# A GNN kernel's fused node pass: straight code for 196 groups on four engines in place of loops of 20 steps

## The reference, cut to what matters

```python
h = jnp.maximum(_layernorm(x, axis=-1), 0.0)
x = x + _L0_gnn_ref(h, edge_index, Ws, att_src, att_dst, bias)    # 3 layers: x + sigmoid(gat_conv(x))
h = jnp.maximum(_layernorm(x, axis=-1), 0.0)
x = x + _L1_gnn_ref(edge_index, h, edge_weight, We0, be0, Wn0, bn0, ...)   # 3 layers
```

## Time and profile before

| what | value |
|---|---|
| time, median of 3 runs | 6525.8 us (6522.49 to 6534.74) |
| time of the profiled execution | 6529.22 us |
| its span, first to last instruction | 6527.7 us |
| busy over the span: PE, DVE, ACT, POOL | 4932.6, 4483.4, 3646.1, 4296.6 us (76, 69, 56, 66%) |
| node pass, 62 to 2007 us: PE, DVE, ACT, POOL busy | 1746.0, 1502.8, 1658.4, 1414.3 of 1945 us |
| granted TensorE clock, mean over the span | 0.878 |

### The profile page before, as it was taken

How to read it: one execution, slowest core, us unless ns; L and a number is a source line. 1 busy time by engine, 2 the same in 40 slices (tenths; PEclk the granted TensorE clock), 3 DMA queues, 4 the chain that set the end, 5 groups by cost and what they waited for, 6 DMA issues and landing times. The chain is left out here.

```text
span 6527.7 us, 110704 instructions
## 1 busy us (share of the span) xinstructions
PE 4932.6 (76%) x23310; PEld 3004.7 (46%) x23310; DVE 4483.4 (69%) x12803; ACT 3646.1 (56%) x7987; POOL 4296.6 (66%) x4317
## 2 busy tenths in 40 slices
PE   4999999999984557847783666059989997776665
PEld 2665555655651134424442444036656664333332
DVE  6887877877865868858885899866655554444443
ACT  4998888988875736645662444753333332333332
POOL 4777777777730077737755775047767775777777
PEclk9999999999998968877886555579999998999998
DMA  6888878777754556646663777877767774444442
GB/s 197 269 277 270 267 261 279 249 223 224 227 185 162 189 149 199 200 126 188 203 203 121 227 231 233 258 212 223 222 202 237 235 234 147 131 129 129 126 124 91
DMA packets 889075, 1314.93 MB, mean 201 GB/s; under 512 B 294247, under 2 KB 347208, under 8 KB 882092
## 3 DMA queue, kind: packets, MB, share of 16 engines
q1 hardware_dynamic: 745906, 1077.42, 49.7%
q0 software_dynamic: 142688, 232.29, 15.1%
HBM read 660.03 MB, written 654.88 MB: 201 GB/s over the span
## 5 line engine op out<-in xcount | busy, mean ns | idle before, releaser
L1304 POOL DMA_INDIRECT g_xs<-table,g_gi x1176 | 1240.1, 1055 | 919.8 <-DMA g_gi<-in_src_lookups_dram 399.4
L1632 POOL DMA_INDIRECT n_xs<-table,n_gi x1176 | 1204.3, 1024 | 727.7 <-DMA n_gi<-lookups 358.2
L1775 DVE TENSOR_TENSOR_SCAN n_dT<-n_km,n_dT,bank 128x512 f32<-128x512 uint8 x291 | 372.4, 1280 | 1007.6 <-PE bank L1660 997.0
L1735 ACT ACTIVATE n_eT<-bank,edge_b 128x512 f32<-128x512 f32 x294 | 202.1, 688 | 803.0 <-PE bank L1677 797.2
L698 PE MATMUL bank<-n_zT,wn 128*128 128x512 f32 (+1 forms) x1176 | 542.7, 597 | 82.9 <-ACT n_sg L756 59.8
L679 PE MATMUL bank<-n_xT,gat_w 128*128 128x512 f32 (+1 forms) x1176 | 561.9, 615 | 54.0 <-issue 34.9
L1643 POOL DMA_INDIRECT out_dram<-n_xn,n_eo x392 | 432.3, 1103 | 124.8 <-issue 113.3
L619 POOL DMA_INDIRECT node_map<-p_es x392 | 401.1, 1023 | 119.5 <-issue 116.5
L647 POOL DMA_INDIRECT p_lk<-node_map,p_gi x392 | 391.3, 998 | 128.2 <-issue 106.1
L1179 DVE CUSTOM_DVE_ANT_0 g_junk<-g_xs,v_src 128x128 f32<-128x128 f32 x1176 | 272.9, 284 | 294.7 <-DMA g_xs<-table,g_gi 293.9
L614 POOL DMA_INDIRECT p_rows<-in_x_dram,p_es x392 | 393.0, 1003 | 124.8 <-issue 113.3
(11 more groups left out here) (253 smaller groups left out, 12292.2 us busy)
## 6 DMA issues: line engine op xcount, KB each, us to landing
table<-n_ro SPq DMA_DIRECT2D x768, 256.0 KB
g_gb<-decays SPq DMA_DIRECT2D x294, 256.0 KB, 4.1
n_xd<-table SPq DMA_DIRECT2D x294, 256.0 KB
table<-g_xn SPq DMA_DIRECT2D x196, 256.0 KB
g_xo<-table SPq DMA_DIRECT2D x196, 256.0 KB
edge_feats<-n_eT SPq DMA_DIRECT2D x196, 256.0 KB, 2.8
table<-n_xn SPq DMA_DIRECT2D x196, 256.0 KB
n_ea<-edge_feats SPq DMA_DIRECT2D x196, 256.0 KB
```

Source lines behind the costliest of these rows:

```text
L1304: q.indirect_dma_start(out=xs[g % XR][:, u, :], out_offset=None, in_=tables[l], in_offset=bass.IndirectOffsetOnAxis(ap=gi[g % 6][:, 0, u:u ...
L1632: q.indirect_dma_start(out=xs[g][:, u, :], out_offset=None, in_=tables[L], in_offset=bass.IndirectOffsetOnAxis(ap=gi[g][:, u, slot_word:sl ...
L1775: V.tensor_tensor_scan(in_order(dT[g][:, :]), kept(g), in_order(flat_banks[1]), 0.0 if begins(g) else carry(dT[g.before(1)]), ALU.mult, AL ...
```

## The change

`unrolled` takes the place of `pipeline` for PE, ACT, DVE and SP in the node pass. It writes all steps out, so that `Turn.i` is None throughout: every address and every count of a wait is a constant, and there is no `Fori`, no branch and no register arithmetic. GpSimd's two pipelines and those of all later passes stay. The parameter `last_peeled` goes. Line numbers behind L80 grow by 10.

```diff
-def pipeline(eng, groups, work, un, base=0, last_peeled=0):
+def pipeline(eng, groups, work, un, base=0):
...
-    turns = (groups - last_peeled - first) // un
+    turns = (groups - first) // un
...
+def unrolled(eng, groups, work, un):
+
+
+    low = min(lag for lag, _ in work)
+    for s in range(groups + max(lag for lag, _ in work) - low):
+        for lag, fn in work:
+            if 0 <= s - lag + low < groups:
+                fn(Turn(None, s - lag + low, un))
...
-                    pipeline(sp, GT, [(-3, load), (5, store(tables[0], h, ln1["done"], h_st)),
+                    unrolled(sp, GT, [(-3, load), (5, store(tables[0], h, ln1["done"], h_st)),
...
-                                      (26, store(out, ro[4], c_rw[2], r_st[4]))], UN, last_peeled=MG)
+                                      (26, store(out, ro[4], c_rw[2], r_st[4]))], UN)
...
-                    pipeline(pe, GT, [(LAG_P[m], product(m)) for m in range(3)]
+                    unrolled(pe, GT, [(LAG_P[m], product(m)) for m in range(3)]
...
-                             + [(22, enter(banks[1], zr, ln2["done"], c_c0, c_t0))], UN, last_peeled=MG)
+                             + [(22, enter(banks[1], zr, ln2["done"], c_c0, c_t0))], UN)
...
-                    pipeline(a, GT, [(1, root(ln1, sc1)), (17, root(ln2, sc2))]
+                    unrolled(a, GT, [(1, root(ln1, sc1)), (17, root(ln2, sc2))]
...
-                    pipeline(v, GT, [(LAG_P[m] + 1, add(m)) for m in range(3)]
+                    unrolled(v, GT, [(LAG_P[m] + 1, add(m)) for m in range(3)]
```

More of the change, by code:

```diff
@@ L775, in _ @@
                              + [(22, enter(banks[1], zT[0], c_t0, c_c0, c_mm[0], 2)),
-                                (21, apply(ln2, sc2, mid, zr, g_st, c_t0))], UN, last_peeled=MG)
+                                (21, apply(ln2, sc2, mid, zr, g_st, c_t0))], UN)
                 @block.vector
@@ L861, in _ @@
                              + [(LAG_ZB[m], zrows_of(m)) for m in range(3)]
-                             + [(1, scales(ln1, sc1)), (17, scales(ln2, sc2))], UN, last_peeled=MG)
+                             + [(1, scales(ln1, sc1)), (17, scales(ln2, sc2))], UN)
         end_phase()
```

## The result

The changed kernel takes 6474.29 us in the median of 6 runs (6470.30 to 6493.45), the kernel before took 6524.09 us on the same chip (6 runs, 6520.94 to 6534.74). The ratio is 0.9925 with an interval of 0.9911 to 0.9939: faster by 0.75%. The forecast was 6472.0 us. The profiled execution took 6474.73 us, 54.5 us less than the profiled one of before; the forecast for such an execution was 6475.4 us.

A forecast was written before the change was run, and what follows sets the result against it. The prediction took TensorE to bound the node pass, with six loop turns as standing time on its path. Removing them, 53.8 us with all other terms nothing, gave 6475.4 us for the profiled execution and 6472.0 us against the median, range 6462 to 6486 us.

The forecast's parts named there:

- What bounds the pass: Node pass: TensorE sets the pace, busy 174.2 of 182.1 us per 20 groups, ScalarE close behind; slow stretches only stand still.
- Term 1: Node-pass loop: six turns back go, 8.7 to 9.4 us each, all on TensorE's path, saving 53.8 us.
- Term 2: PE in the node pass: 12 more waits a group for both holders of a bank cost nothing, bound 0.6 us.
- Term 3: Node-pass sequencers: removed register work ran beside busy engines and gains nothing, bound 0.6 us.
- Term 4: Instruction fetch in the node pass: traffic falls, straight code needing one block in 23.7 us; effect nothing.
- Term 5: Node-pass transfers: same order, DMA keeps up at 0.85 busy; the one disturbed stretch of 41.9 us stays.
- Term 6: GpSimd in the node pass: it keeps its loops, and 79 us of cover remain behind its last stores.
- A: Node pass: pauses have a cause straight code shares, such as a store backlog; only 1.5 us gained, 6524 us; chance 0.02.
- B: TensorE's straight code: each 16 KB block is waited for, 143 us in all, so slower at 6615 us; chance 0.03.
- C: DMA queues in the node pass: a store backlog every 20 groups takes back 33 us, giving 6505 us; chance 0.06.
- D: Later loops: moved code makes a body be refetched, costing 50 us, giving 6522 us; chance 0.01.

The follow-up runs named there:

- e12: Changed kernel with only PE put back into its loop of 20 steps, on the faster chip: 6524.17 us, ratio 1.0007 to the kernel before.
- e2: Changed kernel with ACT, DVE and SP put back into their loops, PE alone straight, on the slower chip: 7995.59 us, ratio 0.9966 to the kernel before.
- e6: Changed kernel without the added waits for the same engine's reader in groups 40 to 179, on the slower chip: 8020.16 us, ratio 0.9945 to the kernel before.
- e10: Changed kernel run again with no edit, on the faster chip: 6471.72 us, ratio 0.9928 to the kernel before.
- e11: Changed kernel with the middle normalisation's and message passes' loops written out too, on the faster chip: 6477.21 us, ratio 0.9933 to the kernel before.
- e8: Changed kernel plus, behind the program, three-pass loops of counted semaphore increments on PE, ACT, DVE and SP: 12229.51 us, which includes these loops.
- e9: Kernel before plus, behind the program, three-pass loops of counted semaphore increments on PE, ACT, DVE and SP: 8965.37 us, which includes these loops.
- e1: Changed kernel with only PE put back into its loop of 20 steps, on the slower chip: 8016.02 us, ratio 1.0000 to the kernel before.

## Why the prediction was right

*What bounds the pass* held. At 182 us for 20 groups PE is busy 174.1 us; with the turns gone nothing else took their place.

*Term 1, six turns, 53.8 us.* Measured 54.4 us at the last row addition. Of the statement that PE's turn is the one on the path and those of ACT, SP and DVE lie beside it, e12 shows the first half: PE's loop alone gives 47.6 us of excess in the trace and the whole in the medians. The prediction reads the parts of a turn, 5.78 us of standing and 2.40 us at the low clock, from the first one alone; over the six turns PE stands for 4.3 to 5.9 us in before and for 3.6 to 6.4 us in e12. The sum didn't rest on that, since it took the stretches. The second half is right while PE has its own turn. If PE has none, as in e2, 2.0 us a turn of the others come to the path, nearly all DVE's (1.9 us); it would be 12 us for six turns. So had only PE been written out, about four fifths of the gain would have come. That is an estimate from two stretches on the slower chip.

*Term 2, waits, nothing:* e6 has the same pace without them. *Term 3, register work, nothing:* the stretch of e12 from 1522 to 1705 us, where PE is in its loop and no turn falls, takes 182.3 us, 0.2 to 0.3 above the straight kernel's; over the 140 steps of the loop that is 2 us at most. *Term 4, fetch of straight code, nothing:* 7 blocks in 166 us, as forecast. PE's idle time from 200 to 1650 us is the 63.2 us of pauses once in a macro group; before had 64.6 us in front of the same products and 32.3 more at the turns. *Term 5, transfers:* DMA share 0.84 to 0.86 while GpSimd gathers, one disturbed stretch of 42.9 us for 41.9, at the place named. *Term 6, GpSimd:* its last stores end 80 us before the last addition; 79 were forecast.

*The rivals.* A falls with the timeline: no engine stands every 20 groups. B falls with eight stretches of 182 us and with PE's pauses, which come every 36.4 us and not at the blocks. C would have shown disturbed stretches away from the last macro group, and there is none. D falls with the equal time behind the node pass (54.4 against 54.5 us). The 108 ns of the Trainium skill (Advanced Engine Details and Errata, Control Flow Timing), by which the change would have been worth nothing, fits neither kind: a kept body's branch shows 208 ns on PE and 45 ns on ACT, a refetched one on PE 3.3 to 3.9 us on the idle core and 6.7 to 8.3 us in before.

*The number.* 6474.29 us is 2.3 us above the forecast and within its range. The kernel before came out 1.7 us lower than the median from which I had started, and the gain of the medians is 49.8 us, 4.0 us less than the sum has. The two profiled executions differ by 54.5 us, 0.7 us more than the sum. So the sum is right to within what the medians scatter: e10's medians differ by 51.2 us, and one of the six runs of the changed kernel took 6493.45 us, 7 us above the range.

## What to carry to other kernels

Look behind every loop's branch: in these traces a branch record of microseconds on TensorE, or a hole of 2.4 us and more between branch and next instruction on the others, at a branch that goes back, came with a body that is fetched anew at every turn. Keep such a body under some 1500 instructions on TensorE and some 250 on ScalarE, VectorE and SyncE, or write it out, first on the engine that sets the pace: its loop alone cost nearly all that there was to win here. A loop whose body is kept gained nothing in total from being written out, as e11 shows: its turns were short already. Whether long turns in a part that is bound by something else cost anything, no run here shows.

## What the hardware showed that I had not expected

- A kept body is smaller than I took for the design of e8: its limit lies between 260 and 350 instructions on ACT, DVE and SP, and between 1550 and 1760 on PE. With blocks of 128 instructions on the three (queue 14 moves 2.20 MB in 269 blocks, 8 KB each) and 256 on PE (queue 8: 2.36 MB in 144 blocks, 16 KB each), the limits fit a body that may touch three blocks on the former and seven on PE, and the dependence on place fits too. The block's length in instructions comes from e8: where DVE alone is left in its long loop a block arrives every 12.2 us at 95 ns an increment, and PE's come every 39.4 us at 154 ns an increment. How many blocks are kept is a reading that no run has tested.
- The branch record of a refetched turn on PE is 3.3 to 3.9 us long when the DMA engines are idle, and 5.8 to 10.0 us in the node pass of three kernels (before, e9, e12), where they are busy to 0.8.
- The pause is followed by a stretch at the lower clock level of 1.2 GHz. In the first turn of before it made up 2.40 of 8.18 us; in e12 it is there as well (4.53 us for the six products, for 2.74). The pauses at turns that I looked at, 3.7 to 5.8 us long, carried this second price, and it goes with them; the pauses of 1.58 us in after don't (the six products behind one take 2.81 us, at a granted clock of 1.00 throughout the stretch).
- The kernel before was 23% slower on another chip in all its runs, with one stretch of 20 groups of e1 at 392.8 us and a DMA share of 0.48, in place of 182 us and 0.84. Straight code on all four engines (e6) was worth 0.55% there, with an interval from 0.25 to 0.84%, and single parts of it could be told only by the late stretches.
